# Second attention: queries made with tokens over partitions, their squares summed on ScalarE, their halves formed from PSUM, and their transposes made by DMA

## The reference, cut to what matters

```
q = (hidden @ q_proj_w.T)   -> 32 heads of 128, rmsnorm over each head's 128, times q_norm_w
k = (ctx @ k_proj_w.T)      -> 8 heads of 128, rmsnorm, times k_norm_w
v = (ctx @ v_proj_w.T)
scores = q k^T / sqrt(128) + mask;  softmax;  times v;  @ o_proj_w.T
rmsnorm(t) = t * rsqrt(mean(t*t) + 1e-5)
```

## Time and profile before

| | |
|---|---|
| median of 3 runs | 2427.87 us (2427.44 to 2430.98) |
| profiled execution | 2430.48 us, its span 2428.6 us, mean granted clock 0.992 |
| TensorE busy | 2371.4 us (98%) |
| VectorE, ScalarE, GpSimd busy | 67%, 52%, 51% |
| share of the DMA queue's packets | 17.3% of 16 engines |
| second attention | from 1366 us to about 2380 us |

### The profile page before, as it was taken

The page is one execution under the profiler, slowest core; times in us unless marked ns, Lnnn a source line. Parts: engine busy times, 40 slices in busy tenths (PEclk is TensorE's granted clock), DMA queues, the critical chain, the costliest instruction groups (busy, mean ns, idle before and its releaser), DMA issues.

```text
span 2428.6 us, 45035 instructions
## 1 busy us (share of the span) xinstructions
PE 2371.4 (98%) x17660; PEld 1298.1 (53%) x17668; DVE 1628.6 (67%) x3133; ACT 1253.3 (52%) x2423; POOL 1228.1 (51%) x983
## 2 busy tenths in 40 slices
PE   8899999999999999999999999999999999999998
PEld 4555555555555555444444655555555555555554
DVE  7977777777777797654443566667666666765666
ACT  7656555555555555423232554555555555544443
POOL 4656666666666666223231455444555555445531
PEclk9899999999999999999999999999999999999999
DMA  6111121112121111011100011122121212221101
GB/s 211 44 45 35 45 53 27 53 27 53 28 56 31 42 40 28 27 44 35 44 11 29 27 31 27 45 53 62 36 62 36 62 36 62 53 43 27 27 14 70
DMA packets 216753, 108.13 MB, mean 45 GB/s; under 512 B 169280, under 2 KB 192480, under 8 KB 216544
## 3 DMA queue, kind: packets, MB, share of 16 engines
q1 hardware_dynamic: 216544, 105.25, 17.3%
HBM read 61.62 MB, written 4.19 MB: 27 GB/s over the span
## 4 chain that ended last, share of the span: by engine, by line
PE 61%; POOL 14%; DVE 11%; issue 4%; ACT 4%; POOLq 0%; DVEq 0%; ACTq 0%
PE PB L865 16%; PE PB L817 14%; PE PB L977 9%; PE PB L801 6%; POOL AR L2710 5%; PE PB L994 5%; POOL AR L2715 4%; POOL PSP L2728 3%; PE PB L907 2%; PE PB L842 2%; DVE AR L2127 2%; DVE WB L1932 2%; PE PB L773 1%; POOL AR L2705 1%; ACT JUNK L1330 1%
## 5 line engine op out<-in xcount | busy, mean ns | idle before, releaser
L865 PE MATMUL PB<-WB,AR 128*128 128x512 f16 x3072 | 687.4, 381 | 3.9 <-DVE X L2142 1.3
L817 PE MATMUL PB<-XTB,WB 128*128 128x512 f16 x3072 | 679.0, 379 | 0.9 <-DVE XTB L1951 0.7
L865 PEld LDWEIGHTS PB<-WB,AR 128*128 128x128 f16 x3072 | 297.5, 98 | 361.8 <-issue 8.0
L817 PEld LDWEIGHTS PB<-XTB,WB 128*128 128x128 f16 x3072 | 297.4, 98 | 344.7 <-issue 4.7
L2721 POOL TENSOR_TENSOR AR<-AR,SML 128x512 f32<-128x512 f32 x128 | 144.8, 1152 | 318.0 <-DVE SML L2112 318.0
L2142 DVE SCALAR_TENSOR_TENSOR X<-PB,SML,X 128x512 f32<-128x512 f32 x256 | 189.4, 747 | 168.7 <-PE PB L865 162.6
L1490 ACT ACTIVATE AR<-PB 128x512 f16<-128x512 f32 x256 | 131.7, 596 | 235.4 <-PE PB L907 235.3
L2022 DVE TENSOR_TENSOR AR<-PB,AR 128x512 f16<-128x512 f32 x128 | 88.2, 690 | 168.0 <-ACT AR L1453 168.0
L2710 POOL TENSOR_TENSOR AR<-AR,CST 128x512 f32<-128x512 f32 x128 | 183.2, 1431 | 33.9 <-ACT AR L1400 33.9
L977 PE MATMUL PB<-XTB,AR 128*128 128x512 f16 (+1 forms) x864 | 192.5, 379 | 0.0
L1406 ACT ACTIVATE AR<-AR 128x512 f16<-128x512 f32 x128 | 80.5, 630 | 206.9 <-POOL AR L2715 205.6
(11 more groups left out here) (273 smaller groups left out, 3785.9 us busy)
## 6 DMA issues: line engine op xcount, KB each, us to landing
STG<-in_wo SPq DMA_DIRECT2D x14, 1024.0 KB
STG<-in_wq SPq DMA_DIRECT2D x13, 1024.0 KB
STG<-in_qw_gu SPq DMA_DIRECT2D x40, 128.0 KB
STG<-in_ctxT SPq DMA_DIRECT2D x4, 1024.0 KB
X<-in_x SPq DMA_DIRECT2D x4, 1024.0 KB, 10.6
out_x<-X SPq DMA_DIRECT2D x16, 256.0 KB, 2.4
STG<-in_wk SPq DMA_DIRECT2D x14, 256.0 KB
STG<-in_wv SPq DMA_DIRECT2D x14, 256.0 KB
```

The costliest lines, as they stand in the source:

```text
L817: m = pe.do.matmul(b[:, :], wq[x][:, k, h * 128:(h + 1) * 128], XT[y][c][:, k, :], start=n == 0, stop=n == 11)
L865: m = pe.do.matmul(b[:, :], AT[x][:, h, t * 128:(t + 1) * 128], wo[y][:, h, :], start=n == 0, stop=n == 11)
```

## The change

A query tile of the second layer becomes 128 tokens by the four heads' 512 columns: queries_1(u, t) has the x half as the stationary operand and the weights as the moving one. For each head ScalarE squares 128 columns with an accumulator; it then scales and adds epsilon (4 columns). GpSimd takes the power of 4 columns. ScalarE writes the high half from PSUM with the norm's factor as a scale a partition, and VectorE writes the low half from PSUM, one instruction a head. Both halves of a tile lie in one block of 1024 fp16 columns, and SP turns them by DMA: tiles 0 and 1 in one transfer, 2 and 3 each in one. Tokens are interleaved in the normalised x (xt_tile, turned_tile), so that a token's batch parity is its position's parity; the stationary operand of the scores, QT_rows, then steps by two elements.

norm_q with its matmuls, its square halves and VectorE's pass over the scores are gone. The keys of units 0 and 1 and P of unit 0 are turned by DMA too. At the start of the layer keys and values of unit 1's second half and of unit 2 stand elsewhere, and the last feed-forward tiles use banks 6, 7, 4, 5. The activation table is loaded ahead of the layer's first work.

```diff
+        QHP = [words(a, 1024, F16) for a in (10752, 5632)]
+        QHL = [QHP[t // 2][:, 1024 * (t % 2):1024 * (t % 2) + 1024] for t in range(4)]
+        QT_tiles = words(0, 2048, F16).rearrange("p (a n) -> p a n", n=128)
+        QT_rows = words(0, 2048, F16).rearrange("p (t a m o) -> p t a m o", t=4, a=4, o=2)
+        def rows_of(L, n, pair, b):
+            if L == 0:
+                return QT[n][:, (pair * BC + b) * 128:(pair * BC + b + 1) * 128]
+            return QT_rows[:, b // 2, 2 * n + pair, :, b % 2]
+        def xt_tile(n, i, c, t):
+            x = XT[n][c][:, :, t * 128:(t + 1) * 128]
+            return x.rearrange("p k (q b) -> p k b q", b=2) if i == 2 else x
...
 sync
+            def turn_q(u, part):
+                first, last = ((0, 2), (2, 3), (3, 4))[part]
+                for t in range(first, last):
+                    sp.wait_ge(q_hi, (1, u, t))
+                    sp.wait_ge(q_lo, (1, u, t))
+                if u > 0:
+                    sp.wait_ge(s_mm, (1, u - 1, 1))
...
+                sp.do.dma_start_transpose(out=QT_tiles[:, 8 * first:8 * last, :],
+                                          in_=QHP[0] if part == 0 else QHL[first]).then_inc(qt_in.of((u, part), 16), 16)
...
+                    elif u < NU - 1:
+                        turn_p_pair(1, u, 0)
+                        turn_q(u + 1, 0)
+                        turn_p_pair(1, u, 1)
+                        turn_q(u + 1, 1)
                         turn_k(u + 1)
+                        turn_q(u + 1, 2)
...
 tensor
+            def queries_1(u, t):
...
+                b = bank(QB[t], (q_hi, (1, u, t)), (q_lo, (1, u, t)))
...
+                        m = pe.do.matmul(b[:, :], XT[x][c][:, k, t * 128:(t + 1) * 128], wq[y][:, k, :],
+                                         start=n == 0, stop=n == 11)
...
+                if L:
                     pe.wait_ge(kt_in, u)
+                    pe.wait_ge(qt_in, (u, 2))
...
-                        if L and t == 1 and not k_by_dma(L, u + 1):
-                            turn_k(u + 1)
-                        if L and t == 2:
-                            norm_q(u + 1)
...
+                    if (L, u) == (1, 0):
+                        keys_values(2, 0)
+                        keys_values(2, 1)
...
             keys_values(0, 0)
+            down(*FFN[-1])
             keys_values(0, 1)
-            down(*FFN[-1])
+            for t in range(4):
+                queries_1(0, t)
             ln_turn(2, 1, 1)
...
 scalar
+            def squares_1(u, t):
...
+                for h in range(4):
+                    n = 4 * t + h
+                    act.do.activation(M1[t][:, 128 * h:128 * h + 128], PB[QB[t]][:, 128 * h:128 * h + 128], ACTF.Square,
+                                      accum_out=RSQ[:, n:n + 1]).then_inc(q_sq.of((u, t)), 1)
+                act.wait_ge(q_sq, (u, t))
+                rs = RSQ[:, 4 * t:4 * t + 4]
+                act.do.activation(rs, rs, ACTF.Identity, scale=1.0 / DH, bias=eco(1, g, 0)).then_inc(q_ms.of((u, t)), 1)
+            def queries_1(u, t):
+                act.wait_ge(q_pow, (u, t))
...
+                for h in range(4):
+                    n = 4 * t + h
+                    act.do.activation(QHL[t][:, 128 * h:128 * h + 128], PB[QB[t]][:, 128 * h:128 * h + 128], copy,
+                                      scale=RSQ[:, n:n + 1]).then_inc(q_hi.of((1, u, t)), 1)
...
+                    for t in range(4):
+                        squares_1(u, t)
+                        if t == 0:
                             halved_p(1, beside)
+                        else:
+                            queries_1(u, t - 1)
+                        if t == 2:
                             halved_k(u)
+                        if t == 3:
+                            queries_1(u, 3)
+                        side(1, beside, 1 + t)
...
 vector
+            def low_1(u, t):
+                dve.wait_ge(q_pow, (u, t))
+                dve.wait_ge(q_hi, (1, u, t))
+                for h in range(4):
+                    n, cols = 4 * t + h, slice(128 * h, 128 * h + 128)
+                    dve.do.scalar_tensor_tensor(QHL[t][:, 512 + 128 * h:640 + 128 * h], PB[QB[t]][:, cols], RSQ[:, n:n + 1],
+                                                QHL[t][:, cols], ALU.mult, ALU.subtract).then_inc(q_lo.of((1, u, t)), 1)
...
-                    dve.do.tensor_tensor(v[pair], by_batch(PB[4 + pair][:, :]),
-                                         RSQ[:, pair * BC:(pair + 1) * BC].unsqueeze(2).to_broadcast([128, BC, SQ]),
-                                         ALU.mult).then_inc(s_out.of((1, u, pair)), 1)
+                    dve.do.scalar_tensor_tensor(v[pair], by_batch(PB[4 + pair][:, :]), PWN[:, 2:3],
+                                                MASK1.unsqueeze(1).to_broadcast([128, BC, SQ]), ALU.mult, ALU.add
+                                                ).then_inc(s_out.of((1, u, pair)), 1)
...
 gpsimd
+            def power_1(u, t):
+                rs = RSQ[:, 4 * t:4 * t + 4]
...
+                pool.do.tensor_tensor(rs, rs, HLF[:, 0:4], ALU.pow).then_inc(q_pow.of((u, t)), 1)
...
+                    for t in range(4):
+                        power_1(u, t)
+                        if t < 2:
+                            halved_p(1, beside, t)
+                        if t == 2:
                             halved_k(u)
+                        side(1, beside, 1 + t)
```

More of the change, by code:

```diff
@@ L868, in output @@
                 m.then_inc(wo_mm.of((L, u, t)), 1)
[L870 to L887, removed]
             def weigh(L, u):
@@ L1149, in front @@
                         values(u)
-                elif u > 1:
+                elif u == 1:
+                    keys_values(1, 1)
+                elif u > 2:
                     keys_values(u, 0)
@@ L1153, in front @@
                 side(L, beside, 0)
-                for h in range(4):
-                    queries(L, u, h)
-                    if (L, beside, h) == (0, 0, 3):
+                for n in range(4):
+                    (queries_1 if L else queries_0)(u, n)
+                    if (L, beside, n) == (0, 0, 3):
                         turn_p(0, 0)
-                    side(L, beside, 1 + h)
+                    side(L, beside, 1 + n)
             def units(L):
@@ L1303, in tensor @@
             keys_values(0, 0)
+            down(*FFN[-1])
             keys_values(0, 1)
-            down(*FFN[-1])
+            for t in range(4):
+                queries_1(0, t)
             ln_turn(2, 1, 1)
-            for h in range(4):
-                queries(1, 0, h)
             keys_values(1, 0)
-            turn_k(0)
-            keys_values(1, 1)
-            norm_q(0)
             units(1)
@@ L2495, in units @@
                             queries_0(u + 1, 2)
-                        if L and t == 1 and not k_by_dma(1, u + 1):
-                            keys_1(u + 1)
-                        if L and t == 2:
-                            norm_q(u + 1)
                         if L == 0 and t == 2:
@@ L2655, in vector @@
             values_1(0, 0)
+            down(*FFN[-1])
             values_1(0, 1)
-            down(*FFN[-1])
+            for t in range(4):
+                low_1(0, t)
             ln_low(2, 1, 1)
-            for h in range(4):
-                queries_1(0, h)
-            keys_1(0)
-            norm_q(0)
+            unit_scale(1, 1)
+            values_1(1, 0)
             units(1)
@@ L2731, in halved_k @@
                 pool.wait_ge(kh, u)
-                if u > 2:
+                if u > 0:
                     pool.wait_ge(kt_in, u - 1)
@@ L2839, in units @@
                     for slot in range(5, 9):
-                        if L and slot == 7:
-                            norm_q(u + 1)
                         side(L, u, slot)
@@ L2895, in gpsimd @@
             keys_1(0)
-            for h in range(4):
-                queries_1(0, h)
-            norm_q(0)
+            for t in range(4):
+                power_1(0, t)
+                if t == 1:
+                    halved_k(0)
             units(1)
```

260 lines of the change are left out of this document (110 added, 150 removed).

## The result

The changed kernel takes 2475.19 us (median of 4 runs, 2472.39 to 2478.64), the one before 2429.43 in the same runs: 1.0195 times as long, 95% interval 1.0183 to 1.0207. I had forecast 2415, and no more than 2438. The profiled execution has a span of 2470.6 us, against 2428.6 before: 42.0 us more.

What follows compares the result with a forecast made beforehand. TensorE, busy 199.91 of 200 us, was taken as the bound. Removing norm_q saved 23.2 us and the layer's start cost 10, so -13 us from the median 2427.9 gave 2415 us, range 2405 to 2438.

Steps and rivals of the forecast that it cites:

- The norm's matmuls: TensorE, second attention: dropping norm_q's 32 one-column matmuls saves 0.80 us a unit, periods 28.9 us in place of 29.7.
- ScalarE's tile: ScalarE's squares, 4-column operation and scaled copies for one query tile: 2.3 us (bounds 2.0 to 2.9), under TensorE's 2.64.
- VectorE's low half: VectorE's four low-half instructions of 286 ns for a query tile: about 1.2 us, in place of one of 0.69.
- The chain to the scores: From a unit's scores through query tiles and transposes: queries land at 28.5 us, needed at 28.9, hidden with 0.4 us cover.
- rival A: Query chain late in every unit: 0.9 us late gives 2429 us, 1.5 us late gives 2447; chance 20%.
- Low half of tile 3: VectorE's last low half ends at 22.9 us, first output addition at 23.7, bank wanted at 25.0: hidden, 1.3 us cover.
- -23.2 + 10 = -13 us: Whole kernel: norm_q's saving less the dearer layer start, net 13 us faster.
- 29 x 0.80: Units 3 to 31: norm_q's matmuls removed 29 times at 0.80 us, 23.2 us less.
- The layer's start: Start of second attention, units 0 and 1: unit 2's scores 10 us later than 1447.20, bounds +4 to +14.
- the three places: TensorE waits at unit 0's scores (some 5 us), its weigh (7 us) and unit 1's output tile 3 (some 8 us).
- signs of being wrong: Forecast wrong if periods exceed 29.3 us, scores last over 2 us, or unit 2's scores come before 1452 or after 1462.
- Rival A's turning point: Lateness of the query chain from which the kernel ends slower than before: about 1.1 us.

Runs made afterwards that it cites:

- e4b: Kernel before with the norm's query sums cut from 32 one-column matmuls to 2 of 16 columns, the rest left out: 2405.30 us, ratio 0.9905.
- e6: Changed kernel with SyncE issuing both transfers of the probabilities ahead of the next unit's first query transfer, in every unit: 2466.60 us, ratio 1.0160.
- e1: Changed kernel with the second attention's side stages given other PSUM banks, and the tail's setup at slots 5 and 7 of unit 25: 2444.85 us, ratio 1.0069.
- e7: e1 with the tail's statistics behind the softmax and its norm, turns and first product later, beside units 27 and 29: 2434.81 us, ratio 1.0028.
- e10: Kernel before with two more ScalarE squares for each query tile of the second attention, inside the chain: 2491.34 us, ratio 1.0257.
- e11: Kernel before with eight extra ScalarE squares a unit, behind all four query tiles: 2435.83 us, ratio 1.0031.
- e3: Changed kernel with one weight tile's scaling and low half beside unit 1 moved from slots 0 to 2 to slots 5, 7 and 8: 2468.95 us, ratio 1.0165.
- e2: Changed kernel with the probabilities' transfers first in unit 0 alone, and VectorE's first output addition ahead of the last low half: 2471.57 us, ratio 1.0177.
- e12: e8 plus the tail's third setup product in bank 1 in place of 6 (e9 without its layer-norm move): 2414.49 us, ratio 0.9943.
- e5: Changed kernel with four repairs together: free banks, later scaling beside unit 1, probabilities' transfers first in every unit, tail's stages moved: 2422.68 us, ratio 0.9980.
- e8: e5 with two half keys_values stages moved earlier in TensorE's order, ahead of unit 0's scores and ahead of weigh(0): 2419.09 us, ratio 0.9963.
- e9: e8 with the layer norm's second turn beside units 2 and 4 one slot later, and the tail's third setup product in bank 1: 2415.21 us, ratio 0.9946.

## Why the prediction was wrong

- **The norm's matmuls, 0.80 us a unit:** right. Calm units fell from 29.74 to 28.93; e4b measured 22.1 us.
- **ScalarE's tile at 2.3 us, VectorE's low half at 1.2:** right. Four squares 1.0, four copies 1.14, four low halves 1.13.
- **The chain to the scores (rival A, 20%):** right up to the landing. Forecast: low half of tile 1 at 18.9, last issue started at 25.4, landed at 28.5. Measured in unit 9: 18.6, 25.4 and 29.7. The double transpose cost 1.91 where I had 2.6, P's behind it 1.72 where I had 1.3; the term that was too small is the landing, 4.3 us where I took the 3.1 of the earlier trace rows, whose longest is 4.3. What makes it 3.1 in unit 10 and 4.3 in unit 9 stays open. The cover was there in most units and missing in five (9, 13, 17, 21 and 24, whose successors' scores wait 0.7 to 1.2 us). e6, which starts the last issue earlier, removed most of that. It is some 5 us of the 42.
- **Low half of tile 3 at 22.9, first addition from there to 23.7:** measured in unit 9 as 22.8 and 23.8. Right, and hidden in calm units.
- **The step that failed: the sum "-23.2 + 10 = -13 us", which has no term for a wait of TensorE in the units with side stages.** The gain in it, "29 x 0.80", was right (e4b); that nothing would be waited for behind it was not. I took one calm unit's timeline for all, and asked of the longer chain only whether scores, weigh and output tile 3 would be met. Seven of the units carry other work whose banks are 1, 2, 3 and 6 and whose readers stand in the same queues. That the chain ends at 22.9 was my own number, and it holds for calm units only (29 in units 27 and 29); that the side stages' banks (TB_TURN, TB_LG, the setup's 6) and VectorE's order hang on it was not looked at. The seven units cost 38.9 us where I had -5.6. The banks (e1, with two slots of unit 25) gave back 30 us, the tail's order (e7) 10 more. That it is the chain's length and not ScalarE's load is shown by e10 against e11.
- **The layer's start, +10 (bounds +4 to +14):** unit 2's scores are 13.5 us later, within the bounds but dearer: waits of 5.2, 8.3 and 7.7 us at the three places that I had named with 5, 7 and 8. Forecast 1457 to 1458, measured 1460.69, between the 1452 and 1462 that I had set as signs of being wrong. Of the 13.5, 2.3 stand ahead of unit 0's scores. e3 shows 5.3 us to be unit 1's scaling; SyncE's order is 2.3 to 2.7 us of unit 0 (e6, e2), and VectorE's first addition 2.1 of the wait in unit 1 (e2 against e6). What is left after e12 is 2.2 us. One sum in it is wrong: from 1384.3 the last tile's terms add up to 1392.3 and not 1392.9, so by my own terms the first wait was 4.4 us.
- **Rival A's turning point** was wrong too: with 0.4 us of cover and 13.2 us to lose over 29 units, the kernel ends slower than before from 0.9 us of lateness on, not 1.1.
- **Units 8 and 23** do not gain: 30.64 and 29.79 us in e12, 30.18 and 29.79 before. e12's timeline has a wait in each that the kernel before has not, for a weight's peak on VectorE (bank 3, as in e10) and for ScalarE's sum of a weight's squares. Both are side work again:

```profile
1652.07 7.94 PE L919 MATMUL PB<-WB,AR 128*128 128x512 f16 x36 [1.29 <-DVE SML L1930]
...
2090.02 0.22 PE L958 MATMUL PB<-IDB,SML 128*128 128x128 bf16 x1 [0.64 <-ACT JUNK L1363]
```

Together with the five above they are why the 22 units gained 9.5 us and not 17.6.
- **What stays open:** why the last landing takes 3.1 us in one unit and 4.3 in another, why units 0 and 1 vary by 2 us and unit 25 by 2.9 without an edit that explains it, and what the repairs would give the kernel before.

## What to carry to other kernels

When a change makes a chain longer on engines off the bound, list what else those engines have queued behind it and who else uses its buffers, in every stage and not only in the loop's calm turn: here seven units lost 39 us, while most calm ones gained their 0.8 as computed. Load on an engine off the bound was free behind the chain in units 2 to 30 (e11), and cost 2.6% inside a chain that holds banks (e10). A bank number or a slot is the cheapest repair; to find it, read the line of the waiting instruction and its releaser, then the releaser's place in its queue.

## What the runs showed of the hardware

- A wait of TensorE can cost more than its length. After 2.83 us of waiting, 24 matmuls of 512 columns took 6.64 us in place of 5.35; after 3.92 us, 48 took 12.21 in place of 10.52; the granted clock from 2300 to 2400 was 0.93, so below the full 2.4 GHz for part of it. In e5, which has not this wait, it was 1.00 there. The extra does not always come: in unit 27 a wait of 2.18 us was followed by twelve matmuls in 2.76 us in e8, and in 4.05 in e9.
- A DMA transpose of 128 x 1024 fp16 took 1.28 us of issue. In unit 9 one of twice that took 1.91 and the one right behind it 1.72; in unit 10 it was 1.99 and 1.65. Issue to landing of the queries' 96 was 3.0 us at least, 3.4 in the middle, 5.3 at most, where P's alone had 3.0, 3.1, 4.3.
